# A transformer block pair on one core: eight instead of six attention maxima beside each of the last 16 projection products

## Chip, cores and metric

The kernel runs on one core of a Trainium2 chip (trn2). The metric is the device time of one execution in microseconds, as the median of several runs. Matrix products run on TensorE (PE in the rows; PEld is its loading of the stationary operand), reductions on VectorE (DVE), activations on ScalarE (ACT), elementwise splits and divisions on GpSimd (POOL). SyncE (SP, in the rows SPq for its queue) issues the DMAs.

## The reference

Two transformer layers on x of 1 x 1024 x 512, each sublayer as x + layernorm(f(layernorm(x))). The part that the change touches is the second attention (the batch in the code is one sequence of S = 1024 tokens, 32 heads of 16 dimensions):

```python
hd = H // HEADS                      # 512 // 32 = 16
qkv = x @ attn_qkvw + attn_qkvb      # (1, 1024, 1536)
q, k, v = ...                        # each (1, 32 heads, 1024, 16)
scores = jnp.einsum('bhqd,bhkd->bhqk', q, k) * scale
probs = jax.nn.softmax(scores, axis=-1)
ctx = jnp.einsum('bhqk,bhkd->bhqd', probs, v)
return ctx @ attn_ow + attn_ob
```

After it come a layer norm, a linear layer with weights of 5-bit codes, and the output.

## The kernel before

Everything of the second attention is in `mha_heads`; the products of the q, k and v projection are in the class `Products`, whose `product`, `store` and so on are called from there.

**Products.** There are 24 (products.COUNT): 16 give q and k in blocks of 128 rows by 512 tokens, 8 give v. Each has four steps (the four 128-row parts of the 512 input features) of three matmuls, since each operand is kept as a high and a low part. q and k go through the DRAM scratch `qk_scratch` to be stacked anew.

**Groups and stacks.** The 32 heads form 8 groups of four. For each group a `q_stack` and a `k_stack` hold 48 rows (high and low parts of the 16 dimensions) of one pair of heads at partition 0 and of the other at partition 64, and a 49th row that carries the negative row maximum. There are buffers for three groups (DEPTH = 3): the stacks of group g lie where those of group g - 3 lay. `load_stacks` loads one group with 12 DMAs of 128 KB. `reload_stacks(g + 2)` is a step of SyncE's loop for g = 1 to 5; it waits until all scores of the group whose buffer it takes are computed, and it stands in SyncE's order behind `put_max(g, 1)` (eight DMAs of maxima rows into q_stack) and `shares.put(g - 1, 1)` (five DMAs of sums and shares out of `ah_out`), which waits for a copy by ScalarE.

**Maxima.** The softmax subtracts the maximum of each row. A "maximum" is one 48-row matmul of 128 queries by 512 keys into one of the three banks of `ah_ring` (`maximum(m)`, L1926) and one reduction by VectorE (`take_one(m)`, L2020). `one_maximum(m)` waits until reduction m - 3 is done, because the bank is used again. There are 64 maxima in a group and 512 in all, in the order of the groups. Successive ones lie on other halves of the array's rows, so two can run beside each other. The first maximum of a group waits for that group's stacks (`stacks_in`).

**Order on TensorE**, written out by hand. First products 2 to 23. `maxima_beside(n, part)` says how many maxima are done behind which part of product n: none up to product 7, then two behind step 0, two behind steps 1 and 2, two behind step 3. That makes FIRST = 96 maxima by the end of the products. Then 128 units (8 groups x 2 halves of the queries x 8 tiles of the keys). A unit has two `scores` (two 49-row matmuls each, L1943) and, behind them, the `mix` of the unit before (eight matmuls, L1958). `maxima_at(unit)` spreads the remaining maxima evenly over the first 116 units:

```python
return min(FIRST - (-unit * (TOTAL - FIRST) // (UNITS - NT - AHEAD)), TOTAL)
```

`maxima_before(n, stage)` places those of a unit: a part before the first scores, a part between the two, a part before the mix. ScalarE takes the exponential of each scores (L1990) and every eight units copies `ah_mix` to `ah_out`. VectorE follows the same plan: with every 32 maxima a `join` and a `turn` (transpose) of their half, and `shares.invert` at the place in the list of maxima that answers to six units after a half's output. SyncE spreads the inverses (L1534, L1538). After the units comes the tail (`mha_tail`).

Of the kernel before, what the change touches and what calls it, by code (L numbers as in the profile page):

```python
# [59 lines left out]
def wait(engine, semaphore, value):  # L60

    if isinstance(value, int) and value <= 0:
        return
    engine.wait_ge(semaphore, value)
# [1658 lines left out]
def mha_heads(nc, io, scratch, later, shares, products, place, finish):  # L1723

    with ExitStack() as ctx:
# [7 lines left out]
        NMAX = NHALF * HALF_MAX  # L1733
        TOTAL = NMAX * GROUPS
        FROM = 8
        FIRST = 6 * (products.COUNT - FROM)
        AHEAD, INVERTED = 4, 6
        STACK_DMAS = 12
        q_stack, k_stack, v = place["q_stack"], place["k_stack"], place["v"]
# [31 lines left out]
        def maxima_at(unit):  # L1771

            return min(FIRST - (-unit * (TOTAL - FIRST) // (UNITS - NT - AHEAD)), TOTAL)

        def maxima_before(n, stage):

            now, then = maxima_at(n), maxima_at(n + 1)
            return (now, min(now + (then - now + 1) // 2, then), min(now + (3 * (then - now) + 2) // 4, then))[stage]

        def maxima_beside(n, part):  # L1780

            return max(6 * (n - FROM) + 2 * (part + 1), 0)

        pieces = {1: (2, 3), 3: (4, 5), 5: (6, 7), 8: (8,), 9: (9,), 10: (10,), 11: (11,)}

# [132 lines left out]
        @block.tensor  # L1918
        def _(pe):
            def maximum(m):  # L1920
                g, n = divmod(m, NMAX)
                t, c, half, p = n // 8, n // 4 % 2, n // 2 % 2, n % 2
                a = g % DEPTH
                if n == 0:
                    pe.wait_ge(stacks_in[a], 16 * (STACK_DMAS * (g // DEPTH + 1) + 2))
                return nc.tensor.matmul(ring[:, m % 3, :], q_stack[a][stack_rows(p, PARTS), c, t * P:(t + 1) * P],  # L1926
                                        k_stack[a][stack_rows(p, PARTS), c, half * BANK:(half + 1) * BANK], start=True, stop=True)

            def one_maximum(m):
                wait(pe, max_taken, m - 2)  # L1930
                maximum(m).then_inc(max_ready, 1)

            def scores(g, u, c, first):
                a = g % DEPTH
                half, j = divmod(u, NT)
                if (g, u, c) == (0, 0, 0):
                    pe.wait_ge(products.v_ready, NT)
                if j == 0 and c == 0:
                    pe.wait_ge(rows_in[half], 16 * 8 * (g + 1))
                wait(pe, probs_ready, 2 * (NUNIT * g + u) + c - 1)  # L1940
                for p in (first, 1 - first):
                    rows = stack_rows(p, PARTS + 1)
                    last = nc.tensor.matmul(score_ps[c][:, p, :], k_stack[a][rows, c, j * P:(j + 1) * P],  # L1943
                                            q_stack[a][rows, c, half * BANK:(half + 1) * BANK], start=True, stop=True)
                last.then_inc(scores_ready, 1)

            def mix(g, u):
                a = g % DEPTH
                half, j = divmod(u, NT)
                if (g, u) == (0, 0):  # L1950
                    pe.wait_ge(ones_set, 1)
                if j == 0:
                    wait(pe, out_taken, NHALF * g + half)
                wait(pe, probs_ready, 2 * (NUNIT * g + u + 1))
                for head in range(4):
                    p, c = divmod(head, 2)
                    rows = slice(32 * head, 32 * head + 32)
                    last = nc.tensor.matmul(mix_ps[rows, :], v[j][:, 4 * g * 2 * HD + 32 * head:4 * g * 2 * HD + 32 * head + 32], probs[:, 2 * (u % 2) + c, p * BANK:(p + 1) * BANK],  # L1958
                                            start=j == 0, stop=j == NT - 1)
                last.then_inc(mixed, 1)  # L1960

            done = 0
            for n in range(2, products.COUNT):
                for part, steps in enumerate(((0,), (1, 2), (3,))):
                    products.product(pe, n, steps)
                    while done < maxima_beside(n, part):
                        one_maximum(done)
                        done += 1
            for n in range(UNITS + 1):
                for stage in range(3):  # L1970
                    while done < maxima_before(n, stage):
                        one_maximum(done)
                        done += 1
                    if n < UNITS and stage < 2:
                        scores(n // NUNIT, n % NUNIT, stage, done % 2)
                    if n and stage == 2:
                        mix((n - 1) // NUNIT, (n - 1) % NUNIT)
            finish_tensor(pe)
# [37 lines left out]
        @block.vector  # L2016
        def _(dve):
            def take_one(m):
                dve.wait_ge(max_ready, m + 1)
                nc.vector.reduce_max(minus_half[:, m:m + 1], ring[:, m % 3, :], AX.X, negate=True).then_inc(max_taken, 1)  # L2020

            def join(b):
                half = b % NHALF
                if b < NHALF:
                    dve.wait_ge(cleared, NHALF)
                dve.wait_ge(max_taken, HALF_MAX * (b + 1))
                wait(dve, rows_ready, b - 1)
                halves = minus_half[:, HALF_MAX * b:HALF_MAX * (b + 1)].rearrange("q (t c two p) -> q t c p two", c=2, two=2, p=2)
                nc.vector.tensor_reduce(minus_max[half][:, 0:16].rearrange("q (c p t) -> q t c p", p=2, c=2), halves, AX.X, ALU.min).then_inc(max_joined, 1)

            def turn(b):
                half = b % NHALF
                dve.wait_ge(max_joined, b + 1)
                wait(dve, rows_in[half], 16 * 8 * (b // NHALF))
                nc.vector.transpose(rows[half][:], minus_max[half][:]).then_inc(rows_ready, 1)

            for half in range(NHALF):
                nc.vector.memset(minus_max[half][:], 0.0).then_inc(cleared, 1)
            m, joined, turned, inverted = 0, 0, 0, 0
            for n in range(products.COUNT + 1):  # L2040
                if n < 4:
                    products.take_first_lower(dve, n)
                until = maxima_beside(n + 1, 2) if n + 1 < products.COUNT else FIRST if n < products.COUNT else TOTAL
                while m < until:
                    take_one(m)
                    m += 1
                    if turned < joined:
                        turn(turned)
                        turned += 1
                    if m - 2 >= HALF_MAX * (joined + 1):  # L2050
                        join(joined)
                        joined += 1
                    if inverted < NHALF * GROUPS and maxima_at(NT * (inverted + 1) + INVERTED) < min(m + 1, TOTAL):
                        shares.invert(dve, inverted)
                        inverted += 1
            for b in range(turned, NHALF * GROUPS):
                if b >= joined:
                    join(b)
                turn(b)
            for b in range(inverted, NHALF * GROUPS - 1):  # L2060
                shares.invert(dve, b)
            finish_vector(dve)


def two_layers(nc, io, out_dram):
    with ExitStack() as ctx:
# [10 lines left out]
        with ExitStack() as first:  # L2077
# [20 lines left out]
            with ExitStack() as layer:  # L2098
# [59 lines left out]
                def finish(ctx, banks, started):  # L2158

                    return mha_tail(nc, ctx, ident, x, later, shares, out_dram, at, banks, started)  # L2160

                mha_heads(nc, io, scratch, later, shares, products, place, finish)


# [60 lines left out]
```

## Time and profile before

| | |
|---|---|
| median of 3 runs | 1574.17 us (1572.78 to 1576.21) |
| the profiled execution | 1572.75 us |
| its span in the trace | 1571.0 us |
| mean granted TensorE clock | 0.973 |
| TensorE busy | 1477.4 us, 94% |
| VectorE busy | 1009.2 us, 64% |
| ScalarE busy | 821.2 us, 52% |

Times in the rows are microseconds from the start of the span, durations too unless marked ns. The products with maxima run from about 1110.7 to 1186, the units from 1186.6 to 1503, the tail to the end.

### The profile page before, as it was taken

To read this page: it belongs to the slowest core of one execution; us is meant where nothing else is said; L and a number is where in the kernel's file an instruction comes from. 1 tells how busy PE (TensorE), PEld (TensorE's weight loads), DVE (VectorE), ACT (ScalarE), POOL (GpSimd) and SP (SyncE) were. 2 spreads that over 40 slices of the span, in tenths; PEclk is the share of its full clock that TensorE was granted. 3 is DMA by queue.
4 is the path that set the end of the run, shared out by engine and by line. 5 is a ranking of instruction groups with operands and counts; after the bars stand their busy time and mean duration, and the time that the engine had idled before them with its cause. 6 is when DMAs were issued, how large, how long until landed. Compare 5 with 4: busy or idle time off the path is not lost. (4 is left out here: it accounts for less than half of the span.)

```text
span 1571.0 us, 22425 instructions
## 1 busy us (share of the span) xinstructions
PE 1477.4 (94%) x8030; PEld 975.8 (62%) x8030; DVE 1009.2 (64%) x1965; ACT 821.2 (52%) x1487; POOL 292.4 (19%) x276
## 2 busy tenths in 40 slices
PE   6866999999999999999979999899999999999998
PEld 4645777767666767767868888787554333333355
DVE  5753666666666666764553334365587999999646
ACT  5325566666666666653212222222315788888854
POOL 2762111111112111100000000001420144443131
PEclk9987999999999999999989999999998999999999
DMA  4142122212122112116322111103840344440001
GB/s 142 54 184 87 49 95 73 71 65 71 65 65 71 65 64 80 33 41 220 107 68 74 61 61 41 54 1 135 201 82 2 62 78 86 74 82 20 18 13 54
DMA packets 63938, 116.57 MB, mean 74 GB/s; under 512 B 13854, under 2 KB 33182, under 8 KB 62542
## 3 DMA queue, kind: packets, MB, share of 16 engines
q1 hardware_dynamic: 63476, 114.23, 25.0%
q10 hardware_dynamic: 288, 0.79, 0.3%
q8 instruction: 65, 1.06, 0.3%
q14 instruction: 45, 0.37, 0.1%
q0 software_dynamic: 64, 0.11, 0.0%
HBM read 82.78 MB, written 29.66 MB: 72 GB/s over the span
## 5 line engine op out<-in xcount | busy, mean ns | idle before, releaser
L2020 DVE TENSOR_REDUCE ah_minus_half<-ah_ring 128x1 f32<-128x512 f32 x512 | 322.7, 682 | 56.2 <-PE ah_ring L1926 52.5
L995 DVE CUSTOM_DVE_ANT_0 mh_score<-mh_score,mh_mask 128x128 f32<-128x128 f32 (+7 forms) x256 | 195.8, 765 | 181.3 <-PE mh_score L806 181.2
L1990 ACT ACTIVATE ah_probs<-ah_score 128x1024 f32<-128x1024 f32 x256 | 247.8, 1023 | 57.9 <-PE ah_score L1943 57.5
L916 ACT ACTIVATE mh_probs<-mh_score,mh_minus_max 128x128 f32<-128x128 f32 (+7 forms) x256 | 189.8, 741 | 40.0 <-DVE mh_minus_max L995 35.9
L1926 PE MATMUL ah_ring<-ah_k_stack,ah_q_stack 48*128 48x512 f32 x512 | 173.7, 458 | 8.6 <-DMA ah_k_stack<-qk_scratch 3.4
L1926 PEld LDWEIGHTS ah_ring<-ah_k_stack,ah_q_stack 48*128 48x128 f32 x512 | 78.8, 187 | 163.2 <-DVE ah_minus_half L2020 150.6
L1070 POOL TENSOR_TENSOR h_lo<-mh_pe,h_hi 64x512 fp32r<-64x512 f32 x64 | 81.8, 1278 | 459.0 <-ACT h_hi L902 455.4
L1943 PE MATMUL ah_score<-ah_q_stack,ah_k_stack 49*128 49x512 f32 x512 | 153.8, 443 | 1.7 <-ACT ah_probs L1990 1.4
L804 PE MATMUL mh_score<-shared,h_hi 128*128 128x512 f32 (+3 forms) x384 | 152.1, 396 | 3.0 <-ACT mh_probs L916 2.9
L1958 PE MATMUL ah_mix<-ah_probs,ah_v 128*32 128x512 f32 x1024 | 139.0, 615 | 0.6 <-ACT ah_probs L1990 0.6
L806 PE MATMUL mh_score<-shared,h_lo 128*128 128x512 f32 (+3 forms) x384 | 133.0, 346 | 0.0
L805 PE MATMUL mh_score<-shared,h_hi 128*128 128x512 f32 (+3 forms) x384 | 131.9, 343 | 0.0
L815 PE MATMUL mh_turn<-ident,mh_probs 128*128 128x128 f32 x672 | 107.7, 277 | 6.5 <-DVE mh_high_turned L1004 6.1
L804 PEld LDWEIGHTS mh_score<-shared,h_hi 128*128 128x128 f32 x384 | 73.1, 190 | 60.5 <-ACT mh_probs L916 36.8
L926 ACT COPY mh_high_turned<-mh_turn 128x128 f32<-128x128 f32 (+3 forms) x128 | 54.6, 427 | 98.3 <-PE mh_turn L820 98.3
L841 PE MATMUL mh_mix<-mh_high_turned,ck 128*64 128x512 f32 (+3 forms) x512 | 102.8, 524 | 0.0
L815 PEld LDWEIGHTS mh_turn<-ident,mh_probs 128*128 128x128 f32 x672 | 75.9, 141 | 27.3 <-issue 23.0
L1004 DVE COPY mh_high_turned<-mh_turn 128x512 f32<-128x512 f32 x128 | 88.0, 687 | 3.1 <-PE mh_turn L815 1.6
L1325 ACT ACTIVATE x<-ff_gate 128x512 f32<-128x512 f32 x28 | 16.7, 598 | 136.3 <-PE ff_gate L1304 136.3
L1943 PEld LDWEIGHTS ah_score<-ah_q_stack,ah_k_stack 49*128 49x128 f32 x512 | 73.3, 188 | 19.5 <-ACT ah_probs L1990 13.5
L1351 DVE TENSOR_TENSOR d<-x,ff_up 128x512 f32<-128x512 f32 x28 | 19.3, 688 | 102.1 <-PE ff_up L1304 102.1
L820 PE MATMUL mh_turn<-ident,mh_probs 128*128 128x128 f32 x480 | 84.0, 273 | 0.0
(238 smaller groups left out, 2870.8 us busy)
## 6 DMA issues: line engine op xcount, KB each, us to landing
mh_w<-in_w_pairs SPq DMA_DIRECT2D x16, 896.0 KB, 5.5
x<-in_w_inner SPq DMA_DIRECT2D x14, 768.0 KB, 4.1
pe_scratch<-fr_pe_out SPq DMA_DIRECT2D x4, 2048.0 KB, 6.6
mh_pe<-pe_scratch SPq DMA_DIRECT2D x16, 512.0 KB, 4.0
mh_spread<-inverse_scratch SPq DMA_DIRECT2D x64, 128.0 KB, 2.9
a_scratch<-mh_mixed SPq DMA_DIRECT2D x32, 256.0 KB, 2.4
x<-a_scratch SPq DMA_DIRECT2D x8, 1024.0 KB, 6.0
qk_scratch<-ai_ring SPq DMA_DIRECT2D x32, 256.0 KB, 2.7
```

The costliest lines, as they stand in the source:

```text
L804: nc.tensor.matmul(out, q_hi[:, i % 2, e, q], m["kt_hi"][e][:, k], start=True, stop=False)
L805: nc.tensor.matmul(out, q_hi[:, i % 2, e, q], m["kt_lo"][e][:, k], start=False, stop=False)
L806: last = nc.tensor.matmul(out, q_lo[:, i % 2, e, q], m["kt_hi"][e][:, k], start=False, stop=True)
L815: last = nc.tensor.transpose(turn_ps[0][:, j, :], probs[:, s % 2, j * P:(j + 1) * P], ident[:])
L841: last = nc.tensor.matmul(mix_ps[e * CR:(e + 1) * CR, q0:BANK], m["ck"][:, j, 0:CR], high_turned[:, j, e, q0:BANK], start=j == 0, stop=j = ...
L916: nc.scalar.activation(probs[:, s % 2, 0:width], score_ps[s % 2][:, base:base + width], ACT.Exp, bias=minus_max[:, s % 4:s % 4 + 1], scale ...
L995: nc.vector.tensor_tensor_reduce(out=scores, in0=scores, in1=mask[:, S - width:S], scale=-1.0, scalar=3e38, op0=ALU.add, op1=ALU.min, accu ...
L1926: return nc.tensor.matmul(ring[:, m % 3, :], q_stack[a][stack_rows(p, PARTS), c, t * P:(t + 1) * P], k_stack[a][stack_rows(p, PARTS), c, h ...
L1943: last = nc.tensor.matmul(score_ps[c][:, p, :], k_stack[a][rows, c, j * P:(j + 1) * P], q_stack[a][rows, c, half * BANK:(half + 1) * BANK] ...
L1958: last = nc.tensor.matmul(mix_ps[rows, :], v[j][:, 4 * g * 2 * HD + 32 * head:4 * g * 2 * HD + 32 * head + 32], probs[:, 2 * (u % 2) + c, ...
L1990: nc.scalar.activation(probs[:, 2 * (u % 2) + c, :], score_ps[c][:].rearrange("p e n -> p (e n)"), ACT.Exp, scale=MHA_SCALE).then_inc(prob ...
L2020: nc.vector.reduce_max(minus_half[:, m:m + 1], ring[:, m % 3, :], AX.X, negate=True).then_inc(max_taken, 1)
```

## The change

Beside each of the products 8 to 23 stand eight maxima instead of six, two behind each of the four steps; steps 1 and 2 become parts of their own. FIRST becomes 128, so the units carry 384 maxima instead of 416, by the same formula. VectorE's list follows. The number of all instructions stays as it is.

```diff
-        FIRST = 6 * (products.COUNT - FROM)
+        FIRST = 8 * (products.COUNT - FROM)
...
-            return max(6 * (n - FROM) + 2 * (part + 1), 0)
+            return max(8 * (n - FROM) + 2 * (part + 1), 0)
...
-                for part, steps in enumerate(((0,), (1, 2), (3,))):
+                for part, steps in enumerate(((0,), (1,), (2,), (3,))):
                     products.product(pe, n, steps)
                     while done < maxima_beside(n, part):
                         one_maximum(done)
...
-                until = maxima_beside(n + 1, 2) if n + 1 < products.COUNT else FIRST if n < products.COUNT else TOTAL
+                until = maxima_beside(n + 1, 3) if n + 1 < products.COUNT else FIRST if n < products.COUNT else TOTAL
```

## Rows read from the trace of the kernel before

**Rows 1.** The page's first part: engine, busy us, share, instructions.
```profile
PE 1477.4 (94%) x8030; PEld 975.8 (62%) x8030; DVE 1009.2 (64%) x1965; ACT 821.2 (52%) x1487; POOL 292.4 (19%) x276
```

**Rows 2.** The page's costliest groups: busy, mean ns | idle before, releaser.
```profile
L1990 ACT ACTIVATE ah_probs<-ah_score 128x1024 f32<-128x1024 f32 x256 | 247.8, 1023 | 57.9 <-PE ah_score L1943 57.5
```

**Rows 3.** Timeline of PE: start, us, engine, line, operation; first, third, fourth pair.
```profile
1123.54 0.49 PE L1926 MATMUL ah_ring<-ah_k_stack,ah_q_stack 48*128 48x512 f32 x2
...
1126.21 0.50 PE L1926 MATMUL ah_ring<-ah_k_stack,ah_q_stack 48*128 48x512 f32 x2
...
1128.24 0.50 PE L1926 MATMUL ah_ring<-ah_k_stack,ah_q_stack 48*128 48x512 f32 x2
```

**Rows 4.** Timeline of DVE, products: six reductions; then a join and a transpose.
```profile
1133.45 3.96 DVE L2020 TENSOR_REDUCE ah_minus_half<-ah_ring 128x1 f32<-128x512 f32 x6 [0.74 <-PE ah_ring L1926]
...
1139.36 0.18 DVE L2029 TENSOR_REDUCE ah_minus_max<-ah_minus_half 128x16 f32<-128x32 f32 x1
1139.48 0.69 DVE L2020 TENSOR_REDUCE ah_minus_half<-ah_ring 128x1 f32<-128x512 f32 x1
```

**Rows 5.** Timeline of PE, starts of units 14, 15 and 16.
```profile
1226.44 0.49 PE L1926 MATMUL ah_ring<-ah_k_stack,ah_q_stack 48*128 48x512 f32 x1
...
1227.57 1.07 PE L1958 MATMUL ah_mix<-ah_probs,ah_v 128*32 128x512 f32 x8
1228.57 0.50 PE L1926 MATMUL ah_ring<-ah_k_stack,ah_q_stack 48*128 48x512 f32 x1
...
1229.85 0.50 PE L1926 MATMUL ah_ring<-ah_k_stack,ah_q_stack 48*128 48x512 f32 x1
...
1231.27 0.50 PE L1926 MATMUL ah_ring<-ah_k_stack,ah_q_stack 48*128 48x512 f32 x1
```

**Rows 6.** Timeline of SyncE's queue, from unit 14 to group 3's reload.
```profile
1227.85 0.34 SPq L1534 DMA_DIRECT2D inverse_mha_scratch<-as_inverse  x1
...
1234.49 0.60 SPq L1516 DMA_DIRECT2D as_sums<-ah_out  x1
...
1238.46 1.52 SPq L1791 DMA_DIRECT2D ah_q_stack<-qk_scratch  x3
...
1242.82 1.35 SPq L1791 DMA_DIRECT2D ah_k_stack<-qk_scratch  x3
```

**Rows 7.** Windows; the last two columns are DMA share and GB/s.
```profile
1245.00:1251.00 6.00, 5.85 (x40) 1.95 (x34) 5.67 (x11) 5.06 (x6) 0.00 (x0) 1.00 1.06 126
1251.00:1252.00 1.00, 1.00 (x10) 0.66 (x7) 0.78 (x2) 0.26 (x1) 0.00 (x0) 1.00 0.43 29
1291.00:1292.00 1.00, 0.91 (x6) 0.43 (x4) 0.97 (x2) 0.73 (x1) 0.00 (x0) 1.00 0.52 45
```

**Rows 8.** Start of unit 30 on PE, and SyncE's queue to group 4's reload.
```profile
1265.81 0.50 PE L1926 MATMUL ah_ring<-ah_k_stack,ah_q_stack 48*128 48x512 f32 x1
...
1275.05 0.59 SPq L1516 DMA_DIRECT2D as_sums<-ah_out  x1
...
1279.05 1.60 SPq L1791 DMA_DIRECT2D ah_q_stack<-qk_scratch  x3
```

**Rows 9.** Timeline of PE, the first maxima; a window, PEclk third last.
```profile
1110.65 0.80 PE L1926 MATMUL ah_ring<-ah_k_stack,ah_q_stack 48*128 48x512 f32 x2 [3.36 <-DMA ah_k_stack<-qk_scratch]
...
1111.00:1114.00 3.00, 3.00 (x8) 1.82 (x6) 1.29 (x2) 0.00 (x0) 0.83 (x1) 0.50 0.87 319
```

**Rows 10.** Scores opening units 1 and 5; a window: its length, PE busy, ..., PEclk third last.
```profile
1188.93 0.64 PE L1943 MATMUL ah_score<-ah_q_stack,ah_k_stack 49*128 49x512 f32 x2
...
1203.89 0.72 PE L1943 MATMUL ah_score<-ah_q_stack,ah_k_stack 49*128 49x512 f32 x2
...
1189.20:1202.80 13.60, 13.60 (x53) 5.21 (x51) 8.27 (x15) 7.04 (x8) 0.00 (x0) 0.50 0.01 1
```

**Rows 11.** SyncE's queue, the last quarter of group 2's stack load.
```profile
1161.27 1.36 SPq L1791 DMA_DIRECT2D ah_k_stack<-qk_scratch  x3
```

## The prediction, on record before the changed kernel ran

> **What bounds the kernel now.** I read the page first. TensorE is busy 94% of the span [rows 1], but that figure says nothing of what a maximum costs, so I went to the costliest groups [rows 2] and then to the timelines of the two stages that the change touches.
>
> Stage one, the 16 products 8 to 23. Between two maxima pairs TensorE runs three or six product matmuls. From one pair to the next but one are 2.67 us, 1.335 each with three product matmuls in between; the gap with six is 2.03 us; a product takes 4.70 us [rows 3]. So a product matmul costs (2.03 - 1.335) / 3 = 0.232 us and a pair 1.335 - 3 x 0.232 = 0.64 us of TensorE's time, although its two matmuls run side by side. VectorE reduces six maxima in 3.96 us, 0.66 each, after 0.74 us idle for the pair [rows 4]. TensorE paces this stage; VectorE is next.
>
> Stage two, the 128 units (four score matmuls, the maxima placed among them, eight mix matmuls). A unit with three maxima goes from 1226.44 to 1228.57 (2.13 us), one with four from 1228.57 to 1231.27 (2.70 us) [rows 5]. The timeline repeats these two lengths, 2.12 and 2.70, in all undisturbed units; I looked through them all. The reason is in the same rows: the fourth maximum starts 1.28 us after the first, because it reuses the first one's ring bank and needs it reduced (0.5 us for the matmul to end, 0.66 us for the reduction, 0.1 us for the signal), and the mix stands behind it. With three maxima the mix starts at 1.13 us. A fourth maximum costs 0.58 us. ScalarE's two activations need 2 x 1.02 us at most per unit [rows 2], below 2.12.
>
> The last 12 units carry no maxima in either kernel and don't change.
>
> **What the change moves.** Before, 96 maxima lie beside the products and 416 among 116 units; after, 128 and 384. By the formula of maxima_at the 116 units were 68 with four and 48 with three; they become 36 and 80. Thirty-two maxima leave a place where each costs 0.58 us for one where each pair costs 0.64 us.
>
> *Products.* One pair more in each of 16: 16 x 0.64 = 10.2 us. Every gap now has three product matmuls, 1.335 us for two reductions of 0.66, so VectorE is busy 1.32 of them. The join and the transpose push it back 0.12 us each [rows 4]; three such places fall into this stage and their delay can no longer drain, about 0.4 us. The first pair's stretch runs at the 1.2 GHz level [rows 9], where the added pair costs some 0.2 us more. Together +10.8 us. Bounds: 10.2 if VectorE keeps up, 13 if each of 64 pairs slips another 0.04 us for a semaphore's latency.
>
> *Units.* 32 x 0.58 = -18.6 us; one of the 32 lies in the slow stretch at the start, where a fourth maximum is worth less: -18.2 us.
>
> *When group 3's data is there.* The maxima now run further ahead of the scores. Maximum 192 is the first of group 3 and needs that group's q and k stacks, which reuse group 0's buffers. Before, it is issued at the start of unit 27; after, in unit 19, between the two score pairs. The reload is SyncE's, in its queue order, and its time hangs on the units, not on the maxima. Before, with T14 = 1226.44 [rows 5]: inverses out at 1227.85, then spread, then eight row DMAs, sums and shares from 1234.49, reload issued from 1238.46 to 1244.2 [rows 6], that is from T14 + 12.0. The sixteen DMA engines are fully busy with it until about 1251.2 [rows 7]. In the changed kernel units 14 and 15 both have three maxima, the output copy that the sums wait for comes a little sooner after T14, and I take 0.2 us off: reload at T14 + 11.8, landed at T14 + 24.6. TensorE reaches maximum 192 at T14 + 4 x 2.12 + 2.70 + 0.5 = T14 + 11.7. It waits **12.9 us**. Queued behind that wait are all scores and mixes, so ScalarE, VectorE and the rest starve as well, and nothing catches up afterwards: TensorE runs in order.
>
> *Group 4.* Maximum 256 goes from unit 44 to the end of unit 38. Its reload ends the same chain, one group on and with two scale loads more in the queue: T30 = 1265.81, sums from 1275.05, reload from 1279.05 [rows 8], last bytes about 1291.3 [rows 7], that is T30 + 25.5. TensorE arrives at T30 + 6 x 2.12 + 2 x 2.70 + 1.28 = T30 + 19.4. It waits **6.2 us**.
>
> *Groups 1, 2 and 5 to 7.* Group 1's stacks are loaded behind products 5 and 7; maximum 64 moves from product 18 to 16, eight products of 5.34 us behind product 8. Group 2's stacks must be there at unit 0. Their loads hang on product 15, and they are issued by 1162.6 [rows 11]; even 5 us later with 7 us to land, as group 3's take from 1244.2 to 1251.2, they come before the products end at about 1197. For group 5 the load lands 25.6 us after unit 46 starts by the same pattern; maximum 320 is due in unit 58, 9 x 2.12 + 3 x 2.70 + 0.4 = 27.6 us after. No wait, 2 us to spare. The later ones have more.
>
> *Clock.* Before product 8's first maximum TensorE waits 3.36 us for a stack; the next 3 us run at a granted clock of 0.50, which is the 1.2 GHz level, and the matmuls there take 0.80 us instead of 0.50 [rows 3, 9]. At the start of the units, at the change from products to units, it falls again and stays at 0.50 for the whole 13.6 us row although TensorE is busy 13.60 of them [rows 10]. Units 1 to 4 take 14.96 us there, 1188.93 to 1203.89 [rows 10], instead of 2 x 2.70 + 2 x 2.12 = 9.64. So a fall inside the unit loop costs 5.3 us. The change adds two waits longer than the 3.36 us one; I count a fall for each, 2 x 5.3 = +10.6 us, and leave the one at the start as it is. Bounds: 2 x 1.5 us if the clock is back after some 3 us of work, half of which is lost, as at product 8, and twice 10.6 if it stays low longer.
>
> The Trainium skill bears on this. Its page "TensorE: Matmul & The Clock Gate" (section "Loop structure matters more than you think") says that a long wait for a DMA between matmuls lets the engine go cold; rows 9 agree. Its section "Terms" prices the loss as throttled time x (1 - K/N), here 13.6 x 0.5 = 6.8 us a fall, an estimate; the units measured 5.3, since part of a unit is not TensorE's. By the page the total would be 3 us higher.
>
> **Sum.** The profiled execution took 1572.75 us (span 1571.0 and 1.75 around it), 1.4 below the median 1574.17 and inside the runs shown. 1572.75 + 10.8 - 18.2 + 12.9 + 6.2 + 10.6 = **1595.0 us**.
>
> **Rivals.**
>
> *A. The reloads are not late (faster).* If stacks 3 and 4 were there in time, only the exchange of places would be left: 10.8 - 18.2 = -7.4, 1565.3 us. It decides at the landing of group 3: earlier than T14 + 11.7 instead of T14 + 24.6. For it: the trace of before has no wait for a stack in the unit loop. Against: the load's last bytes come at 1251.2, twenty microseconds after unit 16 begins, and no part of its chain depends on the maxima; it would have to come 13 us sooner. Chance 4%. One small stall in place of two would give within 0.2%: 2%.
>
> *B. Both waits, clock nearly free, or the second wait small.* Clock costs 2 x 1.5 and not 10.6: 1587.4; with a second wait of 4 us as well: 1585. For it: behind the wait at product 8 the clock was low for some 3 us only. Against: that work was full-height product matmuls; in the unit loop it took 13.6 us. 19%.
>
> *C. Clock slow to return, or VectorE as the new pace of the products.* Units with three maxima hold less matmul work than those with four, and the stretches after the waits consist mostly of them. If each fall lasts twice as long: 1605.6; with the product stage at its upper bound of 13 us: 1608. For it: VectorE has 0.02 us to spare in 1.335. 17%.
>
> *D. Forecast as summed,* between about 1588 and 1603: 58%.
>
> **How the numbers follow.** The likeliest is D, 1595.0. The range 1584 to 1608 holds D, B and most of C, and leaves out A and the tail of C. A measurement here tells 0.2%, 3.1 us, from no change. Faster by more: 4%. Within: 2%. Slower: 94%.
>
> **What would show it.** In the trace after: TensorE idle for about 13 us in unit 19 with the stack's DMA as releaser, and about 6 us in unit 38; product pairs 1.335 us apart, products of 5.34 us; units still 2.12 and 2.70 us long, with 36 of the longer; a granted clock of 0.50 behind each wait; maxima of groups 5 to 7 without a wait. The prediction is wrong if the reload is issued or lands earlier relative to unit 14 than before, if a unit with three maxima behind another is longer than 2.12 us, or if a product takes much more than 5.4 us.

## The result and the profile after

| | before | after |
|---|---|---|
| median | 1573.47 us (1572.5 to 1576.21, 4 executions) | 1619.84 us (1616.67 to 1626.28, 4 executions) |
| ratio | | 1.0297, 95% interval 1.0261 to 1.0333 |
| profiled execution | 1572.75 us, span 1571.0 | 1618.1 us, span 1616.2 |
| mean granted TensorE clock | 0.973 | 0.948 |

The kernel is 3% slower. The forecast was slower too, 1595.0, but half of the loss was missing from it and the time lies above the range. The two profiled executions differ by 45.3 us. Where they lie, from the starts of the first pair of maxima, of unit 0 and of unit 127:

| stretch | before | after | difference |
|---|---|---|---|
| start to the first pair of maxima | 1110.65 | 1112.61 | +2.0 |
| products with maxima | 75.9 | 110.1 | +34.1 |
| unit 0 to unit 127 | 313.1 | 322.2 | +9.1 |

The first two windows of the kernel after show its product stage in two halves, the last two the work behind the first two waits in the units (columns: window, its length, PE busy, PEld, DVE, ACT, POOL, granted clock, DMA share, GB/s). Rows 9 and 10 hold the same view of before.

```profile
1112.60:1172.40 59.80, 59.79 (x130) 28.98 (x130) 33.69 (x54) 9.62 (x16) 12.88 (x11) 0.50 0.43 114
1172.50:1222.70 50.20, 49.97 (x187) 24.92 (x187) 48.10 (x79) 7.26 (x13) 7.37 (x13) 1.00 0.30 54
...
1255.00:1261.00 6.00, 6.00 (x25) 1.84 (x24) 3.25 (x6) 2.96 (x3) 0.00 (x0) 0.50 0.00 0
1289.00:1295.30 6.30, 6.30 (x27) 1.68 (x25) 3.36 (x7) 2.96 (x3) 0.00 (x0) 0.50 0.00 0
```

For 59.8 us TensorE is busy all the time and runs at a granted clock of 0.50, the 1.2 GHz level. The timeline of its pairs shows what that costs. First the beginning of the stage, which answers to [rows 9], then a piece of its second half, which answers to [rows 3]:

```profile
1112.61 0.79 PE L1926 MATMUL ah_ring<-ah_k_stack,ah_q_stack 48*128 48x512 f32 x2 [4.94 <-DMA ah_k_stack<-qk_scratch]
...
1114.91 0.79 PE L1926 MATMUL ah_ring<-ah_k_stack,ah_q_stack 48*128 48x512 f32 x2
...
1200.52 0.50 PE L1926 MATMUL ah_ring<-ah_k_stack,ah_q_stack 48*128 48x512 f32 x2
...
1201.86 0.50 PE L1926 MATMUL ah_ring<-ah_k_stack,ah_q_stack 48*128 48x512 f32 x2
```

Pairs lie 2.30 us apart at 1.2 GHz and 1.34 us at 2.4. Twenty-six of the 64 gaps are long: 26 x 0.96 = 25 us. With the 16 added pairs, 10.2 us, less 1.5 us for the short slow stretch that before had here too [rows 9], that makes 33.7 of the 34.1.

Where nothing waits in the units and the clock is at 1.00, the lengths are those of [rows 5], 2.12 us with three maxima and 2.70 with four, and by the plan 36 of 116 are of the longer kind. TensorE waits three times. Its timeline, at units 11, 19 and 38:

```profile
1254.02 0.79 PE L1926 MATMUL ah_ring<-ah_k_stack,ah_q_stack 48*128 48x512 f32 x1 [5.03 <-DVE ah_minus_half L2020]
...
1288.62 0.76 PE L1926 MATMUL ah_ring<-ah_k_stack,ah_q_stack 48*128 48x512 f32 x1 [13.38 <-DMA ah_k_stack<-qk_scratch]
...
1342.16 0.76 PE L1926 MATMUL ah_ring<-ah_k_stack,ah_q_stack 48*128 48x512 f32 x1 [6.45 <-DMA ah_k_stack<-qk_scratch]
```

The second and third are the forecast waits for the stacks of groups 3 and 4. The first was not in the forecast. VectorE's timeline and SyncE's queue at that place:

```profile
1247.37 0.68 DVE L2020 TENSOR_REDUCE ah_minus_half<-ah_ring 128x1 f32<-128x512 f32 x1
1253.18 0.21 DVE L2035 STREAM_TRANSPOSE ah_rows<-ah_minus_max 128x32 f32<-128x32 f32 x1 [5.14 <-DMA ah_q_stack<-ah_rows]
```

```profile
1244.53 0.61 SPq L1516 DMA_DIRECT2D as_sums<-ah_out  x1
1245.18 2.48 SPq L1519 DMA_DIRECT2D as_c<-ah_out  x4
1247.71 4.39 SPq L1812 DMA_DIRECT2D ah_q_stack<-ah_rows  x8
```

VectorE has joined the maxima of group 2's first half and must transpose them into a row tile. The eight DMAs that still have to read that tile for group 1 went out only at 1247.71, because in SyncE's queue they stand behind the sums and shares, and those wait for the copy that ScalarE makes when unit 8 is through, at 1243.91. The transpose waits 5.14 us, the reductions queue behind it, the ring fills, TensorE stops, and with it ScalarE.

The units add up. 32 maxima x 0.58 = -18.6; units 11 and 12 took 8.78 and 4.16 us instead of 2.12 and 2.70, +8.1; units 19 and 20 took 17.13 and 3.82 instead of 2.70 and 2.12, +16.1; units 38 and 39 took 10.19 and 2.94, +8.3; the slow stretch at the start of the units [rows 10] is missing after, -5.3, and unit 1 is 0.2 longer. Sum +8.8, measured +9.1.

### The profile page after: what moved, and what is told of

Its sections match the earlier page's. It is cut to its first block and busy times, and to the rows that moved or that the text cites. A ratio compares the mean times of both kernels' runs of the same rounds, so it can differ in the third digit from the quotient of the medians.

```text
span 1616.2 us, 22425 instructions
## 1 busy us (share of the span) xinstructions
PE 1500.6 (93%) x8030; PEld 984.4 (61%) x8030; DVE 1011.2 (63%) x1965; ACT 821.3 (51%) x1487; POOL 292.4 (18%) x276
## 5 line engine op out<-in xcount | busy, mean ns | idle before, releaser
L815 PEld LDWEIGHTS mh_turn<-ident,mh_probs 128*128 128x128 f32 x672 | 75.9, 141 | 27.4 <-issue 23.0
L1351 DVE TENSOR_TENSOR d<-x,ff_up 128x512 f32<-128x512 f32 x28 | 19.3, 688 | 102.2 <-PE ff_up L1304 102.2
L1943 PEld LDWEIGHTS ah_score<-ah_q_stack,ah_k_stack 49*128 49x128 f32 x512 | 68.8, 188 | 22.7 <-ACT ah_probs L1990 14.7
```

What stands on the lines that cost most here:

```text
L815: last = nc.tensor.transpose(turn_ps[0][:, j, :], probs[:, s % 2, j * P:(j + 1) * P], ident[:])
```

## Experiments

The theory after the result, here called density: the clock falls at the wait, and it comes back later where fewer product matmuls lie between the pairs. The rivals: the longer wait (4.94 us for 3.36), or chance, kept it low. Then the three waits in the units, each undone by itself. In all kernels but the changed one the count of maxima beside a product is a list, `BESIDE`, for products 8 to 23, and a product with eight has four parts, one with six the three of before.

### Two products at six behind the wait

```diff
-        FIRST = 8 * (products.COUNT - FROM)
+        BESIDE = [6] * 2 + [8] * 14
```

> The changed kernel, but the first two products behind the wait (8 and 9) keep six maxima each, with six product matmuls between the second and third pair; the other 14 have eight (FIRST 124). Theory density: behind the wait the clock comes back only where enough product matmuls lie between the pairs, so it is back within one to seven us as in the kernel before, the 61 us at the 1.2 GHz level shrink to under 10, and the time falls by about 24 us to some 1594. Rival chance: the low clock of the changed kernel hangs on the longer wait ahead of it (4.94 instead of 3.36 us) or on chance, not on what follows; then it stays low for tens of us here too and the time is within 5 us of 1618.

Measured: 1596.16 us in one execution. The wait ahead of the first pair was 5.94 us, longer than in the changed kernel. The gap with six product matmuls is the first one, between the first and the second pair, and not the one that the expectation names. The timeline of the first pairs, and two windows:

```profile
1114.57 0.80 PE L1934 MATMUL ah_ring<-ah_k_stack,ah_q_stack 48*128 48x512 f32 x2 [5.94 <-DMA ah_k_stack<-qk_scratch]
...
1118.15 0.76 PE L1934 MATMUL ah_ring<-ah_k_stack,ah_q_stack 48*128 48x512 f32 x2
...
1119.74 0.50 PE L1934 MATMUL ah_ring<-ah_k_stack,ah_q_stack 48*128 48x512 f32 x2
```

```profile
1111.00:1130.00 19.00, 15.43 (x53) 8.34 (x53) 11.35 (x18) 3.66 (x7) 7.70 (x7) 0.82 0.90 193
1130.00:1150.00 20.00, 20.00 (x77) 10.04 (x75) 19.33 (x33) 5.96 (x10) 7.70 (x6) 1.00 0.50 165
```

After one gap with six product matmuls the matmuls of a pair are back to 0.50 us, and the clock stays at 1.00 while products with eight maxima follow. The product stage took 85.6 us instead of 110.1. The length of the wait is out as the reason, and products with eight maxima keep the 2.4 GHz level here once it is granted. Chance is not out: "Reload first as well" below has a stretch as short with eight maxima from the first product on.

### Four products at eight in the kernel before

```diff
-        FIRST = 6 * (products.COUNT - FROM)
+        BESIDE = [8] * 4 + [6] * 12
```

> The kernel before, but products 8 to 11 have eight maxima, two behind each step; the other 12 keep six (FIRST 104). Theory density: the clock stays low for just these four products, 16 gaps of 2.30 us = 37 us, and comes back at product 12 or 13; that costs 16 x 0.965 = 15 us, with 4 pairs x 0.64 and 8 x 0.58 less in the units about 1586 us in all. Rival chance: low for about 3 us as before, about 1571 us.

Measured: 1580.91 us in one execution, 5 below the expectation (the slow stretch at the start of the units took 3.4 us here, for 13.6 before). The wait ahead of the first pair was 2.38 us, shorter than before. The clock:

```profile
1111.00:1130.00 19.00, 19.00 (x43) 9.19 (x42) 11.46 (x18) 3.54 (x6) 6.79 (x6) 0.51 1.03 243
1130.00:1150.00 20.00, 20.00 (x47) 10.07 (x46) 10.43 (x18) 3.54 (x6) 5.08 (x4) 0.53 0.15 58
1150.00:1170.00 20.00, 20.00 (x78) 10.93 (x77) 16.73 (x27) 5.37 (x9) 7.17 (x8) 1.00 0.28 105
```

Low from 1111.4 to about 1149, 37.5 us for an expected 37, and back in the first gap with six product matmuls. The product stage is 16.9 us longer than before. With eight maxima at its head the kernel before gets the long slow stretch of the changed one, behind a wait shorter than its own.

### The product stage alone

```diff
+        BESIDE = [8] * 16
...
-            return min(FIRST - (-unit * (TOTAL - FIRST) // (UNITS - NT - AHEAD)), TOTAL)
+            return max(FIRST, min(96 - (-unit * (TOTAL - 96) // (UNITS - NT - AHEAD)), TOTAL))
```

> The product stage of the changed kernel (eight maxima each, 128 in all), but from unit 9 on the maxima follow the plan of the kernel before; units 0 to 8 have nearly none. Theory: the waits in units 11, 19 and 38 come from the maxima's running ahead of the scores, so all three are gone, and the product stage keeps its 34 us. Units 0 to 8 take about 18 us. In all about 1599 us. Rival: the waits come from the longer product stage (later stores and loads); then they stay, and the time is 1615 or more.

Measured: 1594.96 us in one execution. All three waits in the units are gone, and behind unit 2 none of the units with maxima is longer than 2.75 us: the waits came from the maxima's running ahead. The stage is slow at first here as well:

```profile
1111.30:1157.20 45.90, 45.90 (x100) 22.22 (x100) 25.97 (x42) 8.36 (x14) 10.92 (x9) 0.50 0.50 131
1157.30:1215.50 58.20, 58.05 (x218) 28.99 (x217) 55.75 (x91) 8.45 (x14) 9.09 (x15) 1.00 0.30 60
```

It took 104.4 us for 110.1, since the slow stretch was 46 us of the stage for 60; that covers the 4 us below the expectation. At this density the clock does come back some time. The four profiles with a long slow stretch (this one, the changed kernel, "Maxima from product 9 on" and "Row DMAs first") have it for 41 to 65 us, and a fifth for 7 ("Reload first as well"); on what that hangs stays open.

### Maxima from product 9 on

```diff
+        BESIDE = [0] + [8] * 15
```

> The changed kernel, but the maxima begin beside product 9 and not 8 (15 products with eight, FIRST 120). Group 0's stacks have landed by then, so TensorE does not idle ahead of the first maximum. Theory density with the wait as its start: no wait, no fall of the clock in the product stage, 15 products of 5.34 us; the waits for groups 3 and 4 shrink to about 9 and 2.5 us, since they are due in units 21 and 40. About 1581 us. Rival: eight maxima a product are too thin to hold 2.4 GHz whatever stands ahead; then some tens of us at 1.2 GHz stay and the time is about 1605.

Measured: 1580.81 to 1610.97 us in eight executions. The lowest is the density theory's figure, 1581. The profiled execution took 1608.72: group 0's stacks came later than I had read off, TensorE waited all the same, and 1.5 us behind the wait the pair's matmuls took 0.79 us:

```profile
1113.66 0.50 PE L1934 MATMUL ah_ring<-ah_k_stack,ah_q_stack 48*128 48x512 f32 x2 [2.98 <-DMA ah_k_stack<-qk_scratch]
...
1115.12 0.79 PE L1934 MATMUL ah_ring<-ah_k_stack,ah_q_stack 48*128 48x512 f32 x2
```

A window of the same run:

```profile
1130.00:1150.00 20.00, 20.00 (x45) 9.68 (x44) 11.36 (x18) 3.83 (x7) 6.24 (x5) 0.50 0.34 121
```

One product later is not late enough to be safe. That the shorter executions had no long slow stretch is seen in no trace, but their mean granted clocks fit it: 0.950 in the profiled execution, whose 65 us at half the clock are 0.020 of its span, and 0.969 and 0.968 in the two shortest, 1581.85 and 1580.81 us. Two at 1587 and 1589 us, with 0.963, lie between. The same kernel has the long stretch in some executions and not in others, so chance has a part in it.

### Row DMAs first in SyncE's queue

```diff
+            put_max(1, 0)
             shares.put(sp, 0, 0, out, out_taken)
-            put_max(1, 0)
```

> The changed kernel with one step moved in SyncE's queue: the eight row DMAs of group 1's first half go out before the sums and shares of group 0's first half and not behind them. Theory: the 5 us wait in unit 11 is VectorE's transpose for group 2, which may not overwrite a row tile before those DMAs have read it; they stood behind a copy that comes only in unit 8. Then the wait is gone, units 11 and 12 take 2.12 and 2.70 us instead of 8.78 and 4.16, the waits in units 19 and 38 stay, and the time is about 8 us lower, 1610. Rival: the wait in unit 11 is for something else in the shares; then it stays.

Measured: 1599.2 us in one execution. Units 11 and 12 took their usual lengths, 2.20 and 2.71 us, so the wait in unit 11 is the row tile's, as argued. The time fell further than expected for two other reasons: the slow stretch of the product stage was 41 us here instead of 61 (102.2 us for the stage, 7.9 less), and the first pair started 5.0 us sooner. The wait for group 3 stayed, 13.77 us, and so did the one for group 4, 7.46 us. The wait ahead of the products was short, and it was still followed by the fall:

```profile
1107.57 0.50 PE L1934 MATMUL ah_ring<-ah_k_stack,ah_q_stack 48*128 48x512 f32 x2 [1.73 <-DMA ah_k_stack<-qk_scratch]
...
1110.94 0.79 PE L1934 MATMUL ah_ring<-ah_k_stack,ah_q_stack 48*128 48x512 f32 x2
...
1268.01 0.76 PE L1934 MATMUL ah_ring<-ah_k_stack,ah_q_stack 48*128 48x512 f32 x1 [13.77 <-DMA ah_k_stack<-qk_scratch]
```

### Reload first as well

```diff
+                if DEPTH <= g + 2 < GROUPS:
+                    reload_stacks(g + 2, range(2))
                 put_max(g, 1)
                 shares.put(sp, g - 1, 1, out, out_taken)
-                if DEPTH <= g + 2 < GROUPS:
-                    reload_stacks(g + 2, range(2))
```

> The kernel of the run above with a second step moved: the reload of group g + 2's stacks goes out before the row DMAs and the shares and not behind them. Theory: the waits in units 19 and 38 are the reload's place in SyncE's queue plus 12.7 us of transfer; it goes out 7 us earlier, so the wait for group 3 falls from 13.8 to about 6 us, the one for group 4 from 7.1 us to none, and the time to about 1593. Rival: the transfer sets the landing (its queue is busy with other loads), the waits stay as they are.

Measured: 1632.93 us in one execution, forty above the expectation. The wait for group 3 did shrink, from 13.77 to 8.00 us (6 expected), so the queue's place does set it. But units 38, 54, 70 and 87 now took 12 to 14 us each, and from unit 0 to unit 127 this kernel needs 358.7 us, 42 more than the run above. The mechanism is plain in the next run.

The product stage of this run bears on density. It is the changed kernel's, eight maxima beside each product from product 8 on, and TensorE waits ahead of it, but its clock came back soon:

```profile
1113.80 0.80 PE L1934 MATMUL ah_ring<-ah_k_stack,ah_q_stack 48*128 48x512 f32 x2 [3.49 <-DMA ah_k_stack<-qk_scratch]
...
1118.40 0.79 PE L1934 MATMUL ah_ring<-ah_k_stack,ah_q_stack 48*128 48x512 f32 x2
...
1120.66 0.50 PE L1934 MATMUL ah_ring<-ah_k_stack,ah_q_stack 48*128 48x512 f32 x2
```

```profile
1113.80:1120.50 6.70, 6.70 (x15) 3.34 (x15) 3.85 (x6) 0.00 (x0) 1.10 (x1) 0.50 0.93 234
1120.60:1201.70 81.10, 80.92 (x303) 40.49 (x302) 77.80 (x127) 16.83 (x28) 20.20 (x23) 1.00 0.43 98
```

Three product matmuls in each gap, and 6.7 us of work at a granted clock of 0.50 instead of 60. The stage took 88.0 us. So the sparse mix does not keep the clock low by itself; it makes a long slow stretch likely. Of the executions with eight maxima from product 8 on, this one escaped it; the profiled one of the changed kernel, "The product stage alone" and "Row DMAs first" had it, and the other three of the changed kernel have mean granted clocks of 0.946 to 0.950, as the profiled one has. Of the kernel before, 33 executions on record lie between 1569.94 and 1579.35 us, so none lost 25 us to it. Density is shown as a matter of odds; what tips a single execution is not known.

### From product 10, both steps moved

```diff
+        BESIDE = [0] * 2 + [8] * 14
```

> Maxima begin beside product 10, eight each (FIRST 112), with both steps of SyncE's queue moved. Theory: no idle ahead of the first maximum, so no fall of the clock and none of its long return; group 3 is due in unit 23 and its stacks land in unit 22, so no wait. The products end within 1 us of the kernel before, the units lose 16 maxima x 0.58 = 9.3 us: about 1563 us, and 5 less where the clock does not fall at the start of the units. Rival: eight maxima a product don't hold 2.4 GHz by themselves; then over 1580.

Measured: 1622.05 us, 1.0302 of before (1.026 to 1.0345), 59 above the expectation. The product stage is right: 74.4 us, no wait, no slow stretch. The loss is in units 39, 55, 71 and 87, at 12 to 14 us, and in the slow stretches behind them. VectorE's timeline in unit 39 and SyncE's queue ahead of it:

```profile
1293.52 0.25 DVE L1529 RECIPROCAL as_inverse<-as_sums 128x16 f32<-128x16 f32 x1 [9.90 <-DMA as_sums<-ah_out]
```

```profile
1267.62 1.50 SPq L1799 DMA_DIRECT2D ah_q_stack<-qk_scratch  x3
...
1277.86 0.59 SPq L1516 DMA_DIRECT2D as_sums<-ah_out  x1
1278.50 8.63 SPq L1519 DMA_DIRECT2D as_c<-ah_out  x4
```

The sums now go out behind 12 stack loads. VectorE's reciprocal needs them, it has a fixed place among the reductions, and it stands 9.90 us with all maxima behind it. From the issue of the sums to the reciprocal are 15.7 us; for the last sums of the same execution, at 1530.22 with no stack load ahead, they are 1.9. In the kernel before the sums go first, and the stacks lose some 4 us that nobody misses there. I had weighed the reload's new place only by who waits for the reload. Behind the wait the unit loop runs at the 1.2 GHz level for 17 us:

```profile
1294.40:1311.40 17.00, 17.00 (x65) 6.63 (x66) 9.76 (x18) 7.43 (x8) 4.72 (x4) 0.50 0.18 49
```

### From product 10, old queue order

> As the run above, with SyncE's queue in the order of the kernel before. Theory: the clock holds in the product stage here too; group 3's stacks land in unit 25 but are due in unit 23, so a wait of some 4 us appears there, with one fall of the clock behind it: about 1569 us. Rival (the queue's order does not matter): the same time as the run above.

Measured: 1569.46 us in one execution, as expected. The timeline shows the wait at group 3, the window the product stage with a granted clock of 1.00 throughout:

```profile
1249.62 0.80 PE L1934 MATMUL ah_ring<-ah_k_stack,ah_q_stack 48*128 48x512 f32 x2 [3.58 <-DMA ah_k_stack<-qk_scratch]
```

```profile
1115.80:1190.20 74.40, 74.17 (x278) 37.06 (x277) 71.41 (x117) 16.75 (x29) 20.21 (x23) 1.00 0.55 128
```

### From product 10, with a bend in the plan

```diff
-            return min(FIRST - (-unit * (TOTAL - FIRST) // (UNITS - NT - AHEAD)), TOTAL)
+            knee = 26
+            if unit <= knee:
+                return FIRST - (-unit * (3 * NMAX - 2 - FIRST) // knee)
+            return min(3 * NMAX - 2 - (-(unit - knee) * (TOTAL - 3 * NMAX + 2) // (UNITS - NT - AHEAD - knee)), TOTAL)
```

> Maxima begin beside product 10, eight each (FIRST 112), SyncE's queue as in the kernel before, and the plan for the units has a bend: 190 maxima by unit 26 and 512 by unit 116, so that group 3 is due in unit 26 or 27 as before; 64 units have three maxima and 52 four, as without the bend. Theory: the wait of the run with an even plan (unit 23 took 7.33 us, unit 24 4.03) is gone and with it its fall of the clock, 5.2 + 1.9 us; 1562 to 1563 us. Rival: the wait comes back at another group, or the even plan's gain was chance; 1569 or more.

Measured: 1565.8 us, 0.9948 of before (0.9935 to 0.996). No unit of the 116 is longer than 2.75 us. Its two windows:

```profile
1115.70:1190.00 74.30, 74.15 (x277) 37.10 (x277) 71.30 (x117) 16.69 (x28) 20.22 (x23) 1.00 0.54 128
1190.10:1489.90 299.80, 293.62 (x1916) 110.22 (x1916) 255.44 (x444) 253.62 (x270) 96.14 (x86) 1.00 0.31 56
```

Some 3 us above the expectation; TensorE reached its first product about 2.4 us later than in the profile of before (1084.61 for 1082.22), ahead of everything that was changed.

### The later start alone

```diff
+        BESIDE = [0] * 2 + [8] * 6 + [6] * 8
```

> The kernel before with the same 96 maxima, but none beside products 8 and 9, eight beside products 10 to 15 and six beside the last eight. The units are as before. Theory: the gain of the later start alone, no wait of 3.4 us and no slow stretch behind it: 4 to 5 us less, about 1568.5. Rival: the wait only moves, since other loads are late; then 1572 or more.

Measured: 1566.49 us, 0.9944 of before (0.9932 to 0.9956), on the same chip as the run above. So both are about 0.5% faster than the kernel before, and between them no difference can be told: the later start brings the gain, and that more maxima beside the products add to it is not shown. In the profiles the two stages together take 374.3 us with 112 maxima and 378.8 with 96; that is 4.5 us, of which 1.0 is a slow stretch in one unit, and it does not show in the medians.

## Why the prediction was wrong, point by point

- **A pair costs 0.64 us in the products:** right. Pairs lie 1.34 us apart in the second half of the stage.
- **VectorE keeps up:** right. It is busy 48.10 of 50.20 us there and the pairs keep their 1.34 us.
- **"The first pair's stretch runs at the 1.2 GHz level, where the added pair costs some 0.2 us more":** this step failed, and it is the larger part of the error. I took the length of that slow stretch from [rows 9] as given, a little over 3 us, and changed only what lies in it. But what lies in it bears on how long it is. With three product matmuls in each gap it lasted 61 us and cost 25. It need not: in the run "Reload first as well" the same stage had 6.8 us of it and took 88.0 us, 12 more than before, close to my +10.8. The odds of a long stretch are what I left out. The rival on the clock (C) had the right idea, that sparser work brings the clock back later, but placed it behind the waits in the units and doubled a price instead of letting it run on.
- **32 x 0.58 us in the units:** right to 0.1 us.
- **The wait for group 3, 12.9 us:** measured 13.4 by the row of the matmuls and 13.8 by that of their weight loads. **For group 4, 6.2:** 6.5 and 6.8 in the same way. **Groups 5 to 7, none:** right.
- **"Groups 1, 2 and 5 to 7" as the only other data to check:** incomplete. I asked for each group when its stacks are there, but not when the row tile that VectorE's transpose overwrites is free. It is on the same path, and the maxima that run ahead reach it in unit 11 instead of unit 18. Missed: 5.4 us of wait and 2.7 of slow clock behind it, 8.1 in all.
- **Two falls of the clock in the units, 2 x 5.3 = 10.6 us:** too dear. Behind the waits the clock was back after 6.7 and 4.4 us of work: 2.3 us lost at units 19 and 20 (16.1 less the 13.8 of the weight loads' row), 1.5 at units 38 and 39 (8.3 less 6.8). The low stretches were 17.1 and 6.8 us long, but a part of each lay in the wait itself and cost nothing. And the fall at the start of the units, 5.3 us, which I left as it was, did not come. Clock in the units, unit 12 apart: -1.5 instead of +10.6. In this execution the falls were short; behind the waits in the units of the other kernels the clock stayed low for 3.6 to 17.1 us of work, so that my 13.6 us lay within what happens. The formula of the Trainium skill's page "TensorE: Matmul & The Clock Gate" (section "Terms") gives more still for the two, (17.1 + 6.8) x 0.5 = 12 us, an estimate. It comes nearer where all of the throttled time is work, as in the product stage: 59.8 x 0.5 = 29.9 us by the page, an estimate, and 25 measured.
- **The sign, and rival A:** the direction was right and for a true reason; the stacks were late by what was worked out. The 6.2 us for group 4 hold a slip of 0.1, since 25.5 - 19.4 is 6.1.

In sum: 22.3 forecast, 45.3 measured. Missing were 23 us in the products, nearly all clock, 8 us in units 11 and 12, 2 us ahead of the first pair and 1 to 2 us of the two waits; 12 us of clock in the units were too much, and without that error, which hid a part of the others, the forecast would have been further off. The 2 us ahead of the first pair are no part of the change: in the profiles of the kernels that begin at product 8 this pair starts anywhere from 1107.57 to 1114.57.

## What to carry to other kernels

When work is spread more thinly over a stretch that begins at the 1.2 GHz level, price that stretch as a range and not by the length it had before: here the same sparse stage had 7 to 61 us of it. Beginning after the wait, so that the stage starts at 2.4 GHz, made the kernel 0.5% faster than before, and none of the four profiles of kernels that do so shows a slow stretch in the products; two products of the old density right behind the wait had a short stretch too, in the one execution there is. When an in-order engine's work is moved ahead, list every wait on its path, also the free-again waits of small tiles on another engine; and before a step is moved forward in a DMA queue, ask who waits for what it is moved past.

## What I had not expected of the hardware

- The same mix of matmuls (three product matmuls and a pair) holds the 2.4 GHz level for 50 to 81 us without a break when it is granted, and where the clock falls at the wait or within 1.5 us behind it, stays at 1.2 GHz for 41 to 65 us in four profiles and for 7 in a fifth. Where the first gap had six product matmuls, the clock was back after 3.4 and 4.2 us of work, in the kernel before and in "Two products at six".
- A wait of 1.73 us ahead of the stage was followed by a fall in one profile; one of 0.52 us was not in another, and neither was, in any of the twelve profiles, an idle time of 1.67 us some 20 us sooner, with product matmuls on both sides of it.
- In the unit loop the clock came back after 4.4 to 7.2 us of work behind the three waits of the changed kernel, and after 3.6 to 17.1 behind those of the other kernels; at the start of the units before it took 13.6 [rows 10]. One such stretch is no price for the next.
- Four share DMAs took SyncE 8.63 us to issue where the stack loads were in front of them, instead of 2.45 to 3.3 us.
